# Sixteen loads of a tile replaced by one load, in an eight-core attention and feed-forward layer

## The chip, the cores and the metric

One Trainium2 chip, all 8 cores, one launch of one program. The time is device microseconds of the slowest core. Each core works alone on its share: core 0 to 3 take the first batch element, 4 to 7 the second, and every core owns 16 blocks of 128 query positions (2048 of 8192, interleaved among the four). Nothing is exchanged between cores; each one computes the keys and values of its whole batch element itself.

## The reference

One post-norm layer on x of shape (2, 8192, 2048): attention with a compressed key/value path, then a feed-forward part with int8 weights.

```
q   = x @ Wq                      # 16 heads of 128 + 64 (the 64 rotated by position)
c   = rmsnorm(x @ Wkv_a[:, :512]) # compressed keys and values
kr  = rope(x @ Wkv_a[:, 512:])    # 64 rotated key values, shared by the heads
k, v = c @ Wkv_b                  # 16 heads of 128 + 128
a   = causal_softmax(q . [k, kr] / sqrt(192)) @ v
x   = layernorm(x + a @ Wo)
g   = silu((x @ w_gate) * s_gate) * ((x @ w_up) * s_up)     # 8192 wide, int8 weights
out = layernorm(x + (g @ w_down) * s_down)
```

## The kernel before

Activations lie transposed: the 2048 features run over 16 chunks of 128 partitions, and 512 positions are the free dimension. A "tile" below is a buffer of 128 partitions x 8192 values in bf16, that is 16 chunks of 512 positions, chunk c in columns 512c to 512c + 511. Products are sums of 16 matmuls over these chunks.

The program has five stages. Each stage ends with a wait of SyncE for every DMA and for VectorE, and the next stage begins on all engines after it.

- A, queries: four input tiles `xb[tt]` (each core's own 2048 positions, from `xq` in f32) stay in SBUF; 24 blocks of query weights `wqb` pass by them. `load_xb` (L321) loads a tile. Tile 0 is loaded ahead of everything, then on the same queue come the casting of the output weights `wo_bf<-wo` (16 copies from DRAM to DRAM), the first query weights, and tiles 1 to 3 (L399). Results go to the scratch tensor `q_scr`.
- B, compressed keys and values: 16 tiles `xb2[par_x]` of the whole sequence (from `xf`, f32, rows of 8192 positions), in two buffers. The load of tile tt (L543) waits until TensorE has finished tile tt - 2, which is the rope block `propeB` of it (L562).
- C, attention: 16 heads by 4 groups of 512 queries. The result of head h and group gq, `ob_sb`, is stored to the scratch tensor `o_scr` (L889).
- D, output projection and first norm: for each gq the 16 heads' results are loaded from `o_scr` as a tile `osb` (L932, L943, from SyncE's queue); `osb` of gq + 1 is loaded at the start of gq once the buffer is free. For each of 16 output blocks weights `wob` and the residual `xtile` are loaded. The sum goes through a norm and to `h1_scr` in f32.
- E, feed-forward: four sweeps sw of 512 positions. Each loads the tile `h1b` from `h1_scr` (L1090, L1138; f32 in DRAM, bf16 in SBUF), runs 64 blocks of gate (L1107) and up (L1113) matmuls against it, then 16 blocks of down matmuls (L1157, 64 matmuls each, weights `wdb`), then transposes, norm and output. The load of `h1b` for the next sweep is written right behind the 64 blocks, waits for their last matmul, and stands in GpSimd's queue ahead of the down weights `wdb` of this sweep.

Loads that cast (all f32 and int8 sources) are issued by GpSimd, in program order; SyncE issues the others, ScalarE the stores to `h1_scr`. `P.dma` (L87) gives each queue four semaphores in turn. Successive DMAs of a queue share one until somebody waits for it; a wait always asks for the count of all DMAs issued on that semaphore so far (L62 to L84). So a wait for one DMA is a wait for the ones issued with it. All DMA issues carry the line of that helper (L101).

Of the kernel before, what the change touches and what calls it, by code (L numbers as in the profile page):

```python
# [9 lines left out]
BF16 = mybir.dt.bfloat16  # L10
# [9 lines left out]
OWN = NSLOT * 128  # L20
# [212 lines left out]
def build_nc(upto=5, dbg=()):  # L233
    nc = bass.Bass("TRN2", target_bir_lowering=False)
    dbg = set(dbg)

    t_xf = nc.dram_tensor("xf", [D, S], F32, kind="ExternalInput").ap()
    t_xq = nc.dram_tensor("xq", [D, OWN], F32, kind="ExternalInput").ap()
# [20 lines left out]
    t_out = nc.dram_tensor("out", [OWN, D], F32, kind="ExternalOutput").ap()  # L259

    q_scr = nc.dram_tensor("q_scr", [3072, OWN], BF16, kind="Internal").ap()
    o_scr = nc.dram_tensor("o_scr", [2048, OWN], BF16, kind="Internal").ap()
    h1_scr = nc.dram_tensor("h1_scr", [D, OWN], F32, kind="Internal").ap()
    wo_bf = nc.dram_tensor("wo_bf", [16, 128, 2048], BF16, kind="Internal").ap()

# [1 line left out]
    def dbg_out(name, shape, dtype):  # L267
        if name in dbg:
            dbg_aps[name] = nc.dram_tensor(
                "dbg_" + name, shape, dtype, kind="ExternalOutput").ap()  # L270
            return dbg_aps[name]
        return None
# [3 lines left out]
    d_krope = dbg_out("krope", [64, S], BF16)  # L276
    d_qmax = dbg_out("qmax", [1, 16], F32)
    d_krn = dbg_out("krn", [1, S], BF16)
    d_oscr = dbg_out("oscr", [2048, OWN], BF16)
    d_h1 = dbg_out("h1", [D, OWN], F32)  # L280
    d_kn15 = dbg_out("kn15", [128, S], BF16)
    d_vt15 = dbg_out("vt15", [128, S], BF16)
# [1 line left out]
    with ExitStack() as g:  # L284
        P = Prog(nc, g)
# [19 lines left out]
        with ExitStack() as a:  # L305
# [13 lines left out]
            pnR = [a.enter_context(nc.psum_tensor(f"pnR{i}", [128, 512], F32)) for i in range(2)]  # L319

            def load_xb(tt):  # L321
                return [P.dma("PL", xb[tt][:, 512 * c:512 * (c + 1)],
                              t_xq[128 * c:128 * (c + 1), 512 * tt:512 * (tt + 1)])
                        for c in range(16)]
            t_xb = {0: load_xb(0)}
            P.dma("SP", cosA[:, :], t_cos_own)
            t_trig = P.dma("SP", sinA[:, :], t_sin_own)
# [51 lines left out]
            for ocb in range(24):  # L379
# [4 lines left out]
                for tt in range(4):  # L384
                    bk = (4 * ocb + tt) % 4
                    par = tt % 2
                    for c in range(16):
                        waits = []
                        if c == 0:
                            waits = [t_w, t_xb[tt][15]] + bank_free[bk] + ([t_sel] if ocb == 0 else [])  # L390
                            bank_free[bk] = []
                        P.op("PE", lambda e, c=c, bk=bk, tt=tt, wpar=wpar: e.matmul(  # L392
                            pq[bk][:, :], wqb[wpar][:, 128 * c:128 * (c + 1)],
                            xb[tt][:, 512 * c:512 * (c + 1)],
                            start=(c == 0), stop=(c == 15)),
                            waits=waits, inc="pe" if c == 15 else None)
# [65 lines left out]
        with ExitStack() as bc:  # L462
# [5 lines left out]
            with ExitStack() as b:  # L468
# [71 lines left out]

                for tt in range(16):
                    par_x = tt % 2
                    t_x = [P.dma("PL", xb2[par_x][:, 512 * c:512 * (c + 1)],  # L543
                                 t_xf[128 * c:128 * (c + 1), 512 * tt:512 * (tt + 1)],
                                 waits=xb_free[par_x])
                           for c in range(16)]
                    xb_free[par_x] = []
                    t_cs = P.dma("SP", cosB[par_x][:, :],
                                 t_cosf[:, 512 * tt:512 * (tt + 1)], waits=cos_free[par_x])
# [4 lines left out]
                    for oc in range(5):  # L554
# [13 lines left out]
                        for c in range(16):  # L568
                            waits = []
                            if c == 0:  # L570
                                waits = [t_x[15], t_wk_ld[15]]
                                waits += (bank_free[par] if oc < 4 else rope_free)
                                if oc < 4:
                                    bank_free[par] = []
                                else:
                                    rope_free = []
                            P.op("PE", mk(c), waits=waits, inc="pe" if c == 15 else None)
# [54 lines left out]
            with ExitStack() as cph:  # L632
# [53 lines left out]
                for h in range(16):  # L686
# [98 lines left out]
                    for gq in range(4):  # L785
# [63 lines left out]
                        for it in range(niter):  # L849
# [27 lines left out]
                            if it % 2 == 1 and it + 3 < niter:  # L877
# [10 lines left out]
                            waits=ob_free[par_g], inc="dve")  # L888
                        ob_free[par_g] = []  # L889
                        po_free[par_g] = [("dve", tok_ob)]  # L890
                        t_ost = P.dma("SP", o_scr[128 * h:128 * (h + 1), 512 * gq:512 * (gq + 1)],
                                      ob_sb[par_g][:, :], waits=[("dve", tok_ob)], cls="st")
                        ob_free[par_g] = [t_ost]
                    kn_free = [("pe", P.cnt["pe"])]
# [15 lines left out]
        with ExitStack() as dph:  # L910
# [18 lines left out]
            osb_free = {0: [], 1: []}  # L929
            r1b_free = []  # L930
            t_o = {}
            t_o[0] = [P.dma("SP", osb[0][:, 512 * c:512 * (c + 1)],  # L932
                            o_scr[128 * c:128 * (c + 1), 0:512])
                      for c in range(16)]
            xt_free = {0: [], 1: []}
            o_free = []
            stat_free = []
# [3 lines left out]
            for gq in range(4):  # L941
                opar = gq % 2
                if gq + 1 < 4:  # L943
                    t_o[gq + 1] = [P.dma("SP", osb[(gq + 1) % 2][:, 512 * c:512 * (c + 1)],
                                         o_scr[128 * c:128 * (c + 1), 512 * (gq + 1):512 * (gq + 2)],
                                         waits=osb_free[(gq + 1) % 2] if c == 0 else ())
                                   for c in range(16)]
                    osb_free[(gq + 1) % 2] = []
                mm_toks = {}
                for oc in range(16):  # L950
# [9 lines left out]
                    for c in range(16):  # L960
                        waits = []
                        if c == 0:
                            waits = [t_o[gq][15], t_w] + bank_free[bk]
                            bank_free[bk] = []
                        P.op("PE", lambda e, c=c, oc=oc, bk=bk, wpar=wpar, opar=opar: e.matmul(  # L965
                            pwo[bk][:, :], wob[wpar][:, 128 * c:128 * (c + 1)],
                            osb[opar][:, 512 * c:512 * (c + 1)],
                            start=(c == 0), stop=(c == 15)),
                            waits=waits, inc="pe" if c == 15 else None)
# [72 lines left out]
        with ExitStack() as eph:  # L1042
# [43 lines left out]
            rtm_free = []  # L1086
            out_free = []
            out_stores = []
            t_h1map = {}
            t_h1map[0] = [P.dma("PL", h1b[:, 512 * c:512 * (c + 1)],  # L1090
                                h1_scr[128 * c:128 * (c + 1), 0:512])
                          for c in range(16)]
            for sw in range(4):
                t_h1 = t_h1map[sw]
                for ic in range(64):
# [4 lines left out]
                    for c in range(16):  # L1100
                        waits = []
                        if c == 0:
                            waits = [t_g, t_h1[15]] + gu_free[par] + (fuse_free if ic == 0 else [])
                            gu_free[par] = []
                            if ic == 0:
                                fuse_free = []
                        P.op("PE", lambda e, c=c, par=par: e.matmul(  # L1107
                            psG[par][:, :], wgb[par][:, 128 * c:128 * (c + 1)],
                            h1b[:, 512 * c:512 * (c + 1)],
                            start=(c == 0), stop=(c == 15)), waits=waits)  # L1110
# [24 lines left out]
                    tu_free[par] = [("dve", tok_f)]  # L1135
                tok_fuse_all = P.cnt["dve"]
                if sw + 1 < 4:
                    t_h1map[sw + 1] = [P.dma("PL", h1b[:, 512 * c:512 * (c + 1)],  # L1138
                                             h1_scr[128 * c:128 * (c + 1), 512 * (sw + 1):512 * (sw + 2)],
                                             waits=[("pe", P.cnt["pe"])] if c == 0 else ())  # L1140
                                       for c in range(16)]
                for oc in range(16):
                    par = oc % 2
                    t_wd_ld = P.dma("PL", wdb[par][:, :], t_wd[oc], waits=wd_free[par])
# [120 lines left out]
```

How the kernel before makes its waits and increments, by code:

```python
                def run(e, ops=ops):  # L124
                    for fn, waits, inc, n in ops:
                        for (s, v) in waits:
                            e.wait_ge(self.sem[s], v)
                        i = fn(e)
                        if inc is not None:
                            i.then_inc(self.sem[inc], n)
```

## Time and profile before

| | us |
|---|---|
| median of 2 runs | 8440.19 |
| lowest and highest of the runs | 8117.09, 8763.28 |
| the profiled execution | 8104.23 |
| its span on the slowest core (core 5) | 8102.7 |
| spans of the 8 cores | 8073.2 to 8102.7 |
| TensorE busy | 6631.2 (82%) |
| VectorE, ScalarE busy | 2568.9, 2592.2 (32% each) |
| GpSimd busy, DMA issues included | 608.3 (8%) |
| bytes moved by DMA | 639 MB, 79 GB/s on average |

Busy time is the time in which an engine had an instruction in work; matmuls overlap, so a busy TensorE isn't one at its peak. "DMA share" is the mean busy share of the core's 16 DMA engines; where several packets of an engine overlap it comes out above 1. GB/s counts the bytes written: a load that casts f32 to bf16 reads twice as much. "PEclk" is the granted TensorE clock, 1.00 for 2.4 GHz and 0.50 for 1.2 GHz.

### The profile page before, as it was taken

The numbers are of one execution on the slowest core, as the hardware profiler recorded it, in microseconds if no ns is written. First come the engines' busy times: TensorE is split into PE (matmuls) and PEld (weight loads), VectorE is DVE, ScalarE is ACT, GpSimd is POOL, SyncE is SP. The second block draws the span as 40 slices with busy tenths as digits, with TensorE's granted clock in tenths as the row PEclk, the third lists the DMA queues.
The fourth block names the chain that finished last, engine by engine and source line by source line (L and its number), as shares of the span: only waits on it lengthen the run. The fifth ranks groups of instructions, "written<-read, shape, count | busy, mean of one in ns | idle before, by whom it ended". The sixth has DMA issues, their size and how long they took to land. (4 is left out here: it accounts for less than half of the span.)

```text
span 8102.7 us, 101785 instructions; the slowest of 8 cores (8073.2 to 8102.7 us)
## 1 busy us (share of the span) xinstructions
PE 6631.2 (82%) x32368; PEld 2786.2 (34%) x32368; DVE 2568.9 (32%) x3876; ACT 2592.2 (32%) x3920; POOL 608.3 (8%) x1161
## 2 busy tenths in 40 slices
PE   3855958888888888888888745598989889988997
PEld 1322423333333333333333212244444444444443
DVE  0154444444444444444444222211021021102112
ACT  0201336555566665555555411000010000001000
POOL 2002400000000000000000001111011101100110
PEclk9977979999999999999999877799999999999999
DMA  8214720000000000000000243444444434443443
GB/s 110 63 31 74 118 44 9 9 7 8 8 9 9 9 8 9 9 9 8 8 9 9 88 128 124 124 154 152 157 144 155 160 140 152 146 171 137 154 162 132
DMA packets 236855, 639.37 MB, mean 79 GB/s; under 512 B 30320, under 2 KB 126704, under 8 KB 225008
## 3 DMA queue, kind: packets, MB, share of 16 engines
q0 software_dynamic: 159568, 530.98, 22.5%
q1 hardware_dynamic: 67552, 85.09, 3.3%
q10 hardware_dynamic: 9216, 16.78, 0.6%
q8 instruction: 277, 4.54, 0.2%
q14 instruction: 242, 1.98, 0.1%
HBM read 453.75 MB, written 62.91 MB: 64 GB/s over the span
## 5 line engine op out<-in xcount | busy, mean ns | idle before, releaser
L826 ACT ACTIVATE ptb<-poolC,bias_sb 128x512 bf16<-128x512 f32 x2560 | 1759.0, 687 | 724.9 <-PE poolC L817 350.0
L833 DVE SCALAR_TENSOR_TENSOR ptb<-qpos_sb,kposc_sb,ptb 128x512 bf16<-128x512 f32 x1024 | 769.2, 751 | 1452.4 <-ACT ptb L826 1366.9
L855 PE MATMUL poC<-ptb,vtm_sb 128*128 128x512 bf16 x2560 | 977.3, 382 | 223.8 <-DVE ptb L833 203.0
L1107 PE MATMUL psG<-h1b,wgb 128*128 128x512 bf16 x4096 | 936.3, 382 | 109.9 <-DMA wub<-wu 84.5
L865 PE MATMUL pdenC<-ptb,ones_mat 128*128 128x512 bf16 x2560 | 968.6, 378 | 0.0
L1157 PE MATMUL psD<-fuse,wdb 128*128 128x512 bf16 x4096 | 890.9, 381 | 65.1 <-DMA wdb<-wd 63.3
L1113 PE MATMUL psU<-h1b,wub 128*128 128x512 bf16 x4096 | 925.8, 379 | 0.0
L1121 ACT ACTIVATE tgE<-psG,sg_sb 128x512 bf16<-128x512 f32 x256 | 175.9, 687 | 1576.0 <-PE psU L1113 1576.0
L1126 DVE TENSOR_SCALAR tuE<-psU,su_sb 128x512 bf16<-128x512 f32 x256 | 192.1, 751 | 1458.3 <-PE psU L1113 1458.3
L1107 PEld LDWEIGHTS psG<-h1b,wgb 128*128 128x128 bf16 x4096 | 401.9, 98 | 604.5 <-issue 131.3
L1157 PEld LDWEIGHTS psD<-fuse,wdb 128*128 128x128 bf16 x4096 | 402.0, 98 | 554.0 <-issue 75.2
L1113 PEld LDWEIGHTS psU<-h1b,wub 128*128 128x128 bf16 x4096 | 400.8, 98 | 483.2
L855 PEld LDWEIGHTS poC<-ptb,vtm_sb 128*128 128x128 bf16 x2560 | 246.1, 96 | 857.7 <-issue 773.4
L813 PE MATMUL poolC<-qr_sb,krope_sb 64*128 64x512 bf16 x1280 | 494.8, 387 | 0.0
L817 PE MATMUL poolC<-qr_sb,krope_sb 64*128 64x512 bf16 x1280 | 494.8, 387 | 0.0
L803 PE MATMUL poolC<-qn_sb,knope_sb 128*128 128x512 bf16 x1280 | 485.3, 379 | 0.0
L810 PE MATMUL poolC<-qn_sb,knope_sb 128*128 128x512 bf16 x1280 | 484.8, 379 | 0.0
L392 PE MATMUL pqA<-xbA,wqb 128*128 128x512 bf16 x1536 | 360.6, 398 | 134.0 <-DMA wqb<-wq 105.2
L965 PE MATMUL pwo<-osb,wob 128*128 128x512 bf16 x1024 | 257.0, 413 | 249.7 <-DMA xtile<-xq 214.8
L1200 ACT ACTIVATE sq<-rtm 128x2048 f32<-128x2048 f32 x16 | 30.6, 1912 | 1038.3 <-DVE rtm L1191 1038.3
L1164 DVE SCALAR_TENSOR_TENSOR r<-psD,sd_sb,h1f 128x512 f32<-128x512 f32 x64 | 48.0, 751 | 905.8 <-PE psD L1157 905.8
L101 POOL DMA_DIRECT2D wob<-wo_bf x64 | 33.8, 528 | 3776.3 <-POOLq L133 3485.7
(137 smaller groups left out, 5428.4 us busy)
## 6 DMA issues: line engine op xcount, KB each, us to landing
wgb<-wg POOLq DMA_DIRECT2D x256, 512.0 KB, 3.4
wub<-wu POOLq DMA_DIRECT2D x256, 512.0 KB, 4.2
wdb<-wd POOLq DMA_DIRECT2D x64, 2048.0 KB, 7.6
xbB<-xf POOLq DMA_DIRECT2D x256, 128.0 KB, 7.0
wob<-wo_bf POOLq DMA_DIRECT2D x64, 512.0 KB, 3.9
xtile<-xq POOLq DMA_DIRECT2D x64, 256.0 KB, 4.3
h_scr<-h1t ACTq DMA_DIRECT2D x64, 256.0 KB, 2.5
h1f<-h_scr SPq DMA_DIRECT2D x64, 256.0 KB, 7.5
```

The lines of the kernel that those rows point to most:

```text
L392: P.op("PE", lambda e, c=c, bk=bk, tt=tt, wpar=wpar: e.matmul(pq[bk][:, :], wqb[wpar][:, 128 * c:128 * (c + 1)], xb[tt][:, 512 * c:512 * ( ...
L803: P.op("PE", lambda e, it=it0, bk=bk0, par_g=par_g: e.matmul(pool[bk][:, :], knope_sb[:, 128 * it:128 * (it + 1)], qn_sb[par_g][:, :], sta ...
L810: P.op("PE", lambda e, it=it1, bk=bk1, par_g=par_g: e.matmul(pool[bk][:, :], knope_sb[:, 128 * it:128 * (it + 1)], qn_sb[par_g][:, :], sta ...
L813: P.op("PE", lambda e, it=it0, bk=bk0, par_g=par_g: e.matmul(pool[bk][:, :], krope_sb[0:64, 128 * it:128 * (it + 1)], qr_sb[par_g][0:64, : ...
L817: tok = P.op("PE", lambda e, it=it1, bk=bk1, par_g=par_g: e.matmul(pool[bk][:, :], krope_sb[64:128, 128 * it:128 * (it + 1)], qr_sb[par_g] ...
L826: tok_e = P.op("ACT", lambda e, bk=bk: e.activation(ptb[bk][:, :], pool[bk][:, :], AF.Exp, bias=bias_sb[:, 0:1], scale=SSCALE), waits=[("p ...
L833: tok_m = P.op("DVE", lambda e, it=it, bk=bk, gq=gq: e.scalar_tensor_tensor(ptb[bk][:, :], qpos_sb[:, 512 * gq:512 * (gq + 1)], kposc_sb[: ...
L855: P.op("PE", lambda e, it=it, bk=bk, par_g=par_g, niter=niter: e.matmul(po[par_g][:, :], vtm_sb[:, 128 * it:128 * (it + 1)], ptb[bk][:, :] ...
L865: tok_pv = P.op("PE", lambda e, it=it, bk=bk, niter=niter: e.matmul(pden[:, :], ones_mat[:, :], ptb[bk][:, :], start=(it == 0), stop=(it = ...
L1107: P.op("PE", lambda e, c=c, par=par: e.matmul(psG[par][:, :], wgb[par][:, 128 * c:128 * (c + 1)], h1b[:, 512 * c:512 * (c + 1)], start=(c ...
L1113: P.op("PE", lambda e, c=c, par=par: e.matmul(psU[par][:, :], wub[par][:, 128 * c:128 * (c + 1)], h1b[:, 512 * c:512 * (c + 1)], start=(c ...
L1157: P.op("PE", lambda e, c=c, par=par: e.matmul(psD[par][:, :], wdb[par][:, 128 * c:128 * (c + 1)], fuse[:, 512 * c:512 * (c + 1)], start=(c ...
```

## The change

The tile loads in A, B, D and E are each written as one `dma_start` with a three-dimensional pattern (partition, chunk, position) in place of sixteen. In D the scratch tensor `o_scr` is laid out anew, group by partition by head by position, so that the part of one partition of a tile is one run of 16 KB. The stores into it keep their shape. The waits stay where they were.

```
-    o_scr = nc.dram_tensor("o_scr", [2048, OWN], BF16, kind="Internal").ap()
+    o_scr = nc.dram_tensor("o_scr", [4, 128, 16, 512], BF16, kind="Internal").ap()
...
             def load_xb(tt):
-                return [P.dma("PL", xb[tt][:, 512 * c:512 * (c + 1)],
-                              t_xq[128 * c:128 * (c + 1), 512 * tt:512 * (tt + 1)])
-                        for c in range(16)]
+                src = t_xq[:, 512 * tt:512 * (tt + 1)].rearrange(
+                    "(c p) q -> p c q", p=128)
+                dst = xb[tt][:, :].rearrange("p (c q) -> p c q", c=16)
+                return [P.dma("PL", dst, src)]
...
-                    t_x = [P.dma("PL", xb2[par_x][:, 512 * c:512 * (c + 1)],
-                                 t_xf[128 * c:128 * (c + 1), 512 * tt:512 * (tt + 1)],
-                                 waits=xb_free[par_x])
-                           for c in range(16)]
+                    t_x = [P.dma("PL", xb2[par_x][:, :].rearrange("p (c q) -> p c q", c=16),
+                                 t_xf[:, 512 * tt:512 * (tt + 1)].rearrange(
+                                     "(c p) q -> p c q", p=128),
+                                 waits=xb_free[par_x])]
...
-                        t_ost = P.dma("SP", o_scr[128 * h:128 * (h + 1), 512 * gq:512 * (gq + 1)],
+                        t_ost = P.dma("SP", o_scr[gq, :, h, :],
                                       ob_sb[par_g][:, :], waits=[("dve", tok_ob)], cls="st")
...
-            t_o[0] = [P.dma("SP", osb[0][:, 512 * c:512 * (c + 1)],
-                            o_scr[128 * c:128 * (c + 1), 0:512])
-                      for c in range(16)]
+            t_o[0] = [P.dma("SP", osb[0][:, :], o_scr[0])]
...
-                    t_o[gq + 1] = [P.dma("SP", osb[(gq + 1) % 2][:, 512 * c:512 * (c + 1)],
-                                         o_scr[128 * c:128 * (c + 1), 512 * (gq + 1):512 * (gq + 2)],
-                                         waits=osb_free[(gq + 1) % 2] if c == 0 else ())
-                                   for c in range(16)]
+                    t_o[gq + 1] = [P.dma("SP", osb[(gq + 1) % 2][:, :],
+                                         o_scr[gq + 1], waits=osb_free[(gq + 1) % 2])]
...
+            def load_h1b(sw, waits=()):
+                src = h1_scr[:, 512 * sw:512 * (sw + 1)].rearrange(
+                    "(c p) q -> p c q", p=128)
+                dst = h1b[:, :].rearrange("p (c q) -> p c q", c=16)
+                return [P.dma("PL", dst, src, waits=waits)]
             t_h1map = {}
-            t_h1map[0] = [P.dma("PL", h1b[:, 512 * c:512 * (c + 1)],
-                                h1_scr[128 * c:128 * (c + 1), 0:512])
-                          for c in range(16)]
+            t_h1map[0] = load_h1b(0)
...
-                    t_h1map[sw + 1] = [P.dma("PL", h1b[:, 512 * c:512 * (c + 1)],
-                                             h1_scr[128 * c:128 * (c + 1), 512 * (sw + 1):512 * (sw + 2)],
-                                             waits=[("pe", P.cnt["pe"])] if c == 0 else ())
-                                       for c in range(16)]
+                    t_h1map[sw + 1] = load_h1b(sw + 1, waits=[("pe", P.cnt["pe"])])
```

The four places that waited for piece 15 of a tile (`t_xb[tt][15]` and its like) now wait for the one load.

## Rows read from the trace of the kernel before

**Rows 1.** Windows A to E: length, busy us by engine, PEclk, DMA share, GB/s.
```profile
0.00:705.00 705.00, 400.25 (x1664) 166.97 (x1664) 235.72 (x443) 96.11 (x161) 55.96 (x115) 0.87 0.37 62
705.00:1060.00 355.00, 303.47 (x1360) 132.49 (x1360) 126.12 (x182) 107.54 (x177) 143.62 (x272) 0.92 0.72 108
1060.00:4552.00 3492.00, 2917.09 (x15648) 1119.32 (x15648) 1575.42 (x2320) 2066.81 (x3105) 2.12 (x4) 0.93 0.04 10
4552.00:5149.00 597.00, 288.15 (x1152) 117.06 (x1152) 136.12 (x197) 93.82 (x149) 68.82 (x130) 0.76 0.40 127
5149.00:8102.00 2953.00, 2722.22 (x12544) 1250.40 (x12544) 495.51 (x736) 227.95 (x328) 337.77 (x641) 0.96 0.43 151
```

**Rows 2.** Who waited for whom: us in total, times, longest us.
```profile
PE pwo L965 <- DMA xtile<-xq: 214.8, 33, 52.1
...
PE pqA L392 <- DMA wqb<-wq: 105.2, 1, 105.2
...
PE psG L1107 <- DMA wub<-wu: 84.5, 9, 75.7
...
PE psD L1157 <- DMA wdb<-wd: 63.3, 3, 21.2
...
PE pkvB L562 <- DMA xbB<-xf: 38.4, 1, 38.4
...
PE pwo L965 <- DMA osb<-o_scr: 33.6, 2, 29.6
...
PE pqA L392 <- DMA xbA<-xq: 28.7, 3, 11.1
```

**Rows 3.** Timeline in stage B: start us, us, instruction.
```profile
762.59 8.45 POOL L101 DMA_DIRECT2D xbB<-xf  x16 [28.73 <-PE propeB L562]
...
775.84 3.64 PE L562 MATMUL propeB<-xbB,wkva_sb 128*64 128x512 bf16 x16
...
780.70 13.99 PE L562 MATMUL pkvB<-xbB,wkva_sb 128*128 128x512 bf16 x64
```

**Rows 4.** Windows over one tile load in stage B.
```profile
766.00:771.00 5.00, 5.00 (x25) 2.26 (x24) 1.36 (x3) 2.06 (x4) 5.00 (x10) 1.00 1.13 154
771.00:778.00 7.00, 7.00 (x33) 3.18 (x32) 0.00 (x0) 2.37 (x4) 0.04 (x1) 1.00 1.16 197
778.00:781.00 3.00, 3.00 (x14) 1.14 (x13) 0.54 (x1) 0.94 (x2) 0.92 (x2) 1.00 0.02 3
```

**Rows 5.** Timeline between the up and the down matmuls of sweep 0.
```profile
5617.52 8.44 POOL L101 DMA_DIRECT2D h1b<-h_scr  x16 [12.75 <-PE psU L1113]
...
5625.82 1.20 POOL L101 DMA_DIRECT2D wdb<-wd  x2
...
5638.01 27.21 PE L1157 MATMUL psD<-fuse,wdb 128*128 128x512 bf16 x119 [21.07 <-DMA wdb<-wd]
```

**Rows 6.** Windows over the same stretch.
```profile
5619.00:5626.00 7.00, 0.00 (x0) 0.00 (x0) 0.00 (x0) 0.00 (x0) 7.00 (x15) 0.59 0.96 132
5626.00:5631.00 5.00, 0.00 (x0) 0.00 (x0) 0.00 (x0) 0.00 (x0) 1.02 (x2) 0.50 1.23 201
5631.00:5641.00 10.00, 2.99 (x8) 1.12 (x9) 0.00 (x0) 0.00 (x0) 0.00 (x0) 0.51 1.07 417
```

**Rows 7.** Groups of instructions: busy us, mean ns, idle before them.
```profile
L101 POOL DMA_DIRECT2D wdb<-wd x64 | 34.2, 542 | 801.3 <-PE psD L1157 785.4 <-issue 16.0
```

**Rows 8.** DMA queue of GpSimd from 5617 to 5643 us: packets, MB, share.
```profile
q0 software_dynamic: 2592, 6.29, 92.5%
```

**Rows 9.** Window in stage A, after the last of its tile loads was issued.
```profile
105.00:120.00 15.00, 6.55 (x16) 2.25 (x16) 0.00 (x0) 2.47 (x3) 0.53 (x1) 0.82 1.13 154
```

**Rows 10.** Window at the start of stage D, while its first loads flow.
```profile
4564.00:4575.00 11.00, 0.00 (x0) 0.00 (x0) 0.00 (x0) 0.00 (x0) 0.00 (x0) 0.50 1.05 342
```

**Rows 11.** The chain that ended last, at the start of stage E.
```profile
5149.27 6.97 POOL h1b L101 x14
...
5171.53 6.09 PE psG L1107 x16
```

More of the change, by code:

```diff
@@ L278, in build_nc @@
     d_krn = dbg_out("krn", [1, S], BF16)
-    d_oscr = dbg_out("oscr", [2048, OWN], BF16)
+    d_oscr = dbg_out("oscr", [4, 128, 16, 512], BF16)
     d_h1 = dbg_out("h1", [D, OWN], F32)
@@ L389, in build_nc @@
                         if c == 0:
-                            waits = [t_w, t_xb[tt][15]] + bank_free[bk] + ([t_sel] if ocb == 0 else [])
+                            waits = [t_w, t_xb[tt][-1]] + bank_free[bk] + ([t_sel] if ocb == 0 else [])
                             bank_free[bk] = []
@@ L570, in build_nc @@
                             if c == 0:
-                                waits = [t_x[15], t_wk_ld[15]]
+                                waits = [t_x[-1], t_wk_ld[15]]
                                 waits += (bank_free[par] if oc < 4 else rope_free)
@@ L962, in build_nc @@
                         if c == 0:
-                            waits = [t_o[gq][15], t_w] + bank_free[bk]
+                            waits = [t_o[gq][-1], t_w] + bank_free[bk]
                             bank_free[bk] = []
@@ L1102, in build_nc @@
                         if c == 0:
-                            waits = [t_g, t_h1[15]] + gu_free[par] + (fuse_free if ic == 0 else [])
+                            waits = [t_g, t_h1[-1]] + gu_free[par] + (fuse_free if ic == 0 else [])
                             gu_free[par] = []
```

## The prediction, made before the changed kernel ran

> **What bounds the kernel now.** I read the busy time by stage first [rows 1]. Five stages follow each other, each closed by a wait for everything: A (queries, 0 to 705 us), B (keys and values compressed, to 1060), C (attention, to 4552), D (output projection and first norm, to 5149), E (feed-forward, to 8102). TensorE is busy for 303 of 355 us in B and 2722 of 2953 us in E, so both are bound by it; C moves only 10 GB/s and has none of the changed loads; D has TensorE busy for 288 of 597 us and waits on other things. DMA is never the long-run bound: its share is 0.72 in B and 0.43 in E. A faster load can therefore only give back time in which TensorE stands still for it. The list of waits [rows 2] says how much there is: 105.2 us for the first query weights, 28.7 us in three waits for the next input tiles, 38.4 us for B's first tile, 33.6 us for the attention output in D, 63.3 us in three waits of 21 us between the two halves of a feed-forward sweep, and 75.7 us ahead of E. Of that last one only the part from 5149 us on is loads: E's loads are issued at 5149.3 us and TensorE starts at 5171.53 [rows 11], 22 us. The whole pool is about 290 us, 3.6% of the span, and most of it is the transfer itself.
>
> **What the change removes.** Every load of a 128 x 8192 tile in 16 pieces becomes one instruction: 4 tiles in A, 16 in B, 4 in E (from GpSimd's queue, f32 read and bf16 written), 4 in D (from SyncE's queue, bf16 both ways). That is 28 x 15 = 420 issues fewer. Bytes and the 2 KB reads of the f32 sources stay. The semaphores are picked and closed at the same points as before, because each wait already covered all 16 pieces. Each piece carries 16 packets beside its 128 rows: around the boundary in E 16 + 2 issues make 2592 packets [rows 8], 144 each, so a tile goes from 2304 to 2064 packets. In D the scratch tensor is laid out so that a partition's 16 KB are one run; the stores into it keep 128 rows of 1 KB.
>
> **GpSimd's issue time.** One piece holds GpSimd for 8.44 / 16 = 0.53 us [rows 3], and so does a down-weight load of 128 rows of 8 KB, 0.54 us [rows 7]: the size in bytes doesn't matter. All its issues have 128 rows, so no row shows what 2048 rows cost. The bounds are 0.53 us (per instruction) and 16 x 0.527 = 8.44 us, today's 16 issues together [rows 3, 5] (per row). It also isn't shown whether the first bytes move while the rest of the rows are still being written, as they do now between pieces. Call G the delay this puts before the first bytes. I take G small, below 3 us: an issue's cost hasn't followed its work so far. I keep 8.44 us for the range.
>
> **Stage B, hidden.** The load of a tile is issued at 762.59 us, when the tile two before it is done, and TensorE needs it at 780.70 us [rows 3]. Data flow from about 764 to 778.1 us: 154 GB/s up to 771, 197 GB/s after it, and a share of 0.02 from 778 on [rows 4]. So 14.1 us of transfer lie under 18.1 us of matmuls with 2.6 us to spare. What hides the load is the tile in between; 14 tiles repeat this (the first two are issued together). With G under 0.53 + 2.6 = 3.1 us nothing changes: 0 us. Without the cover every us of G costs 14 us. The first tile, behind the 16 loads of `wkva_sb` in the queue, is waited for: 0 to 10.4 - 14.1 = -4 us by the rates above and below, I take -1.
>
> **Stage E, exposed.** At the end of a gate/up half 16 pieces are issued from 5617.52 us, the first down weights at 5625.82 us, and TensorE starts at 5638.01 us after 21.07 us [rows 5]. The down weights share the queue and the semaphore with the 16 pieces, so TensorE waits for both. The engines move 132 GB/s during the issues, 201 GB/s from 5626 to 5631 us, then 417 GB/s, which are the down weights [rows 6]; the 2.1 MB tile is through at about 5631.4 us. The queue is backed up, not starved: a piece of 128 KB in 0.527 us would be 249 GB/s. Were the whole tile moved at 201 GB/s, it would take 10.4 us in place of 12.5: -2.1 us. Were the low rate the memory's, as in A, where 154 GB/s flow with GpSimd issuing only one load [rows 9], nothing is won. I take -1 us at each of four places (three boundaries and the start of E), -4 us together; bounds 0 and -8.4.
>
> **Stage A.** The queue is full: TensorE starts at 105.2 us behind the casting of the output weights and waits for the next three tiles [rows 2]. The load moves at 154 GB/s [rows 9] long after the last issue. Fewer packets: 0 us, at best 3 x 4 = 12 us off if these tiles ran at 201 GB/s (14 against 10.4 us). A large G would delay the very first bytes once: up to +8 us.
>
> **Stage D.** TensorE's first start waits for two attention tiles and the first weights, 5.8 MB, which flow at 342 GB/s in the steady part with 1 KB rows [rows 10]. With 16 KB rows at the best read rate seen (2 x 201 = 402 GB/s, since f32 is read for bf16) 4.2 MB take 10.4 us in place of 12.3: -2 us, bounds 0 and -4. The second wait for such a tile is 33.6 - 29.6 = 4.0 us [rows 2]; behind it TensorE waits up to 52.1 us for `xtile`, whose load waits for the norm's vector work, and that doesn't move: 0 us, bounds 0 and -4.
>
> **Sum.** B -1, E -4, A 0, D -2: -7 us. The profiled execution took 8104.2 us (span 8102.7), so 8097 us. The runs shown are 8117.1 and 8763.3 us; their median 8440.2 us is the mean of an undisturbed and a disturbed run, and I forecast the undisturbed time. Lower bound: -4 -8 -12 -8 = -32 us, 8072 us, and 13 us for the gap of 8104 to 8117 taken downwards: 8059.
>
> **Rivals.** *Late start, slower inside 2%.* The queue's rows are written one by one and the transfer starts only after the last: G = 8.44 us, 7.9 us more than now. In B the tile ends at 786.0 us, 5.3 us late; if the rate is then 201 GB/s throughout, 1.7 us late. Times 14: 24 to 74 us. TensorE then stands still long enough for its clock to fall as at the boundaries (0.50 in [rows 6]; the first 16 matmuls take 6.09 us [rows 11] where a quarter of 13.99 us [rows 3] is 3.50), up to 14 x 2.6 = 37 us more. E: 4 x (7.9 less 0 to 3.6) = 17 to 32; A and B's start 0 to 16. In all +41 to +159 us, middle +90: 8194 us. For it: the cost of one issue could be all rows. Against it: the cost of an issue has not moved with anything yet. It turns into a loss at G above 3.1 us.
>
> *Long generation, slower over 2%.* The same with rows that cost more in a three-dimensional pattern: each further us of G costs 14 (B) + 4 (E) + 2 = 20 us. At G = 20 us this is 90 + 11.6 x 20 = +320: 8424 us. It passes 2% (162 us) from G of about 12 us, 5.9 ns a row, where 527 ns / 128 = 4.1 ns is the most that today's issues can hold. No row speaks for it.
>
> *Slow reads, slower over 2%.* A DMA engine now reads 16 rows that lie 128 rows apart (4 MB apart in B's source, 1 MB in the others) where it read neighbours, and these fall on the same part of memory; the rate halves. B: 10.4 us become 20.8, or 14.1 become 28.2: 4.2 to 11.5 us late, x 14 = 59 to 161, clock up to 37. E: 4 x 10.4 to 14 = 42 to 56; A the same; B's first 10 to 14. +153 to +324, middle +220: 8324 us. Against it: across the 16 engines the rows read at one moment are spread as before. The Trainium skill (DMA: Bandwidth & Descriptors, Latency and other measured facts) has the rule behind this: copies whose rows are 4 MiB apart ran at half the rate of those 512 KiB apart. By it only B's source would suffer, +69 to +212 us from the terms above for B. No row here has such a stride.
>
> *Faster over 2%.* Each piece pays for its own start and end on the engines. The most the rows allow is 14.1 - 10.4 = 3.7 us at nine exposed tiles (A 4, B 1, E 4), 33 us: 8071 us. Over 2% would need 162 of the 290 us of waits. The Trainium skill (DMA: Bandwidth & Descriptors, Anatomy of one DMA and Rules for kernel authors) asks for coalescing, since a load costs about 2.0 us plus its bytes; by that, as an estimate from the page, 16 pieces of 256 KB would cost 42 us and one load 11.6 us, and nine such tiles would give 270 us back. The trace disagrees for loads queued together: [rows 4] have all 16 pieces through in 14 us.
>
> **How the numbers follow.** No change beyond small gains 0.50; late start 0.27; other shifts inside 2% 0.04; slow reads 0.09; long generation 0.08; faster over 2% 0.02. The likeliest gives 8097 us, with its own range 8059 to 8125. Small gains, late start and other shifts are the cases within 2% (about what a measurement of this kernel can tell from no change): 0.81. Slower by more 0.17, faster by more 0.02. The range takes the cases within 2%, from 8059 to 8104 + 159 = 8263 us.
>
> **What would show it.** GpSimd's span of one tile load against 8.44 us; TensorE's waits in B for the tile load (none if I am right, 14 of 2 to 6 us in the late start); the start of data after the issue, and the rate in B against 154 and 197 GB/s (about 100 with slow reads); the three waits for the down weights at 19 to 21 us, or near 28; D's first wait for `osb` at 26 to 30 us. A tile load with a span above 3.1 us before its first bytes, or a rate near 100 GB/s in B, would make the forecast wrong.

## The result, and the profile after

| | before | after |
|---|---|---|
| runs compared, us | 8096.4, 8103.1, 8111.6, 8117.1 | 8166.8, 8167.2, 8172.1, 8177.0 |
| profiled execution, span of the slowest core, us | 8102.7 (core 5) | 8175.4 (core 0) |
| spans of the 8 cores, us | 8073.2 to 8102.7 | 8124.9 to 8175.4 |

The ratio is 1.0079, 95% interval 1.0061 to 1.0096: the changed kernel is slower by 0.8%, about 64 us. The forecast was 8097 us and no change beyond small gains; 8170 us lie within 2% and within its range, but it is the sign that went wrong, and the runs below are about that. The times named are those of executions in which no die ran at a lower granted clock than the other, and the others (medians over all 8647.8 and 8491.4 us) say nothing here. One more execution of the changed kernel on record, 8157.0 us, isn't among those compared; with it the difference would be 61 us.

For every run below I took, core by core, the time from GpSimd's first instruction in a stage to its first in the next. The table has the median over the 8 cores of the profiled execution, in us:

| | A | B | C | D | E |
|---|---|---|---|---|---|
| before | 706.5 | 357.4 | 3487.8 | 579.3 | 2955.3 |
| after | 704.1 | 426.0 | 3488.8 | 576.2 | 2946.8 |
| difference | -2.4 | +68.6 | +1.0 | -3.1 | -8.5 |

The whole loss is in stage B. E gives a little back. D's length depends on how the cores happen to be staggered when they reach it: from core to core it took 567 to 593 us before and 568 to 602 us after.

The profile after, where it answers to the rows of before. First, who waited for whom on TensorE (columns: us in total, times, longest us), beside [rows 2]:

```profile
PE pwo L962 <- DMA xtile<-xq: 248.3, 34, 48.6
...
PE pqA L393 <- DMA wqb<-wq: 101.8, 1, 101.8
...
PE pkvB L563 <- DMA xbB<-xf: 99.9, 8, 47.9
...
PE psG L1107 <- DMA wub<-wu: 81.4, 5, 73.6
...
PE psD L1154 <- DMA wdb<-wd: 59.3, 3, 19.8
...
PE pqA L393 <- DMA xbA<-xq: 27.7, 3, 9.6
```

All are a little shorter but two. TensorE waits 99.9 us in eight waits for B's tiles where it waited once, 38.4 us (over the 8 cores 84.7 to 99.9 us, before 35.2 to 38.4). Its wait for `osb` is gone from core 0's list, and what it waits for at D's start, some 20 us, is now called `xtile`. So only the sum of the two compares: 248.4 us before on core 5, 248.3 us after on core 0, and 239 against 234 us as medians of the 8 cores.

The timeline of stage B, beside [rows 3] (start us, us, instruction, in brackets the wait before it):

```profile
765.94 1.15 POOL L101 DMA_DIRECT2D xbB<-xf  x1 [53.24 <-PE propeB L563]
...
783.43 1.14 POOL L101 DMA_DIRECT2D xbB<-xf  x1 [16.34 <-PE propeB L563]
...
789.46 16.35 PE L563 MATMUL pkvB<-xbB,wkva_sb 128*128 128x512 bf16 x63 [5.35 <-DMA xbB<-xf]
...
927.60 15.56 PE L563 MATMUL pkvB<-xbB,wkva_sb 128*128 128x512 bf16 x63 [11.75 <-DMA xbB<-xf]
```

The load is issued in 1.15 us, not 8.45, and yet TensorE starts 23.5 us after its issue where it had started after 18.1, having waited 5.35 us. Other tiles wait up to 12 us, and the matmuls of the four blocks after a wait take 16.35 in place of 13.99 us, at a granted clock of 0.88 (the window from 790 us below).

Windows over the same stretch, beside [rows 4] (length, busy us by engine, PEclk, DMA share, GB/s):

```profile
770.00:790.00 20.00, 14.60 (x65) 6.36 (x65) 6.27 (x10) 5.78 (x10) 1.14 (x1) 0.94 1.01 110
790.00:808.00 18.00, 17.95 (x74) 7.65 (x73) 2.31 (x4) 4.73 (x8) 0.00 (x0) 0.88 0.92 107
812.00:824.00 12.00, 11.95 (x57) 5.40 (x57) 6.40 (x9) 3.58 (x7) 0.00 (x0) 1.00 1.14 167
```

This is where the time went. The DMA engines are about as busy as before (share about 1) but move 107 to 110 GB/s in place of 154 to 197. What an engine has in work takes longer, for the same bytes and the same rows of 2 KB. And the rate isn't always low: for one tile, from 812 to 824 us, it is 167 GB/s. The rates of one core also vary with what the others move (last section), so the cleanest comparison is the stretch in which all 8 cores load their first two tiles. Core 0 from 724 to 740 us, before, after, and in the run e3_pad that follows below:

```profile
724.00:740.00 16.00, 4.88 (x15) 1.90 (x16) 0.00 (x0) 0.00 (x0) 5.42 (x11) 0.54 1.15 159
724.00:740.00 16.00, 0.00 (x0) 0.00 (x0) 0.00 (x0) 0.00 (x0) 0.00 (x0) 0.50 1.07 111
724.00:740.00 16.00, 4.41 (x12) 1.70 (x13) 0.00 (x0) 0.00 (x0) 0.00 (x0) 0.51 1.16 167
```

Over the 8 cores it is 157 to 171 GB/s before and 104 to 117 after: the rate is down by a third.

How long each tile load takes from issue to landing, minimum, median and maximum in us, after:

```profile
L101 POOL DMA_DIRECT2D xbB<-xf x16: 1140/1142/1300, 710.3 to 1067.4; - x16
...
DMA to landing us min/median/max: 18.8/27.9/48.8
```

The same for the tile of stage E, whose rows lie 1 MB apart:

```profile
L101 POOL DMA_DIRECT2D h1b<-h_scr x4: 1157/1158/1205, 5227.4 to 7164.2; - x4
...
DMA to landing us min/median/max: 13.7/14.0/15.8
```

Same shape in SBUF, same bytes, same issue cost, half the time (in E the cores don't all load at once, so the distance isn't the only difference). Last, the boundary in E, beside [rows 5] and [rows 6]:

```profile
5691.57 1.16 POOL L101 DMA_DIRECT2D h1b<-h_scr  x1 [13.06 <-PE psU L1113]
5692.72 1.08 POOL L101 DMA_DIRECT2D wdb<-wd  x2
5710.81 29.41 PE L1154 MATMUL psD<-fuse,wdb 128*128 128x512 bf16 x120 [19.85 <-DMA wdb<-wd]
```

The windows over it (columns as above):

```profile
5692.00:5702.00 10.00, 0.00 (x0) 0.00 (x0) 0.42 (x1) 0.00 (x0) 1.80 (x3) 0.69 1.01 158
5702.00:5712.00 10.00, 1.19 (x3) 0.43 (x4) 0.00 (x0) 0.00 (x0) 0.00 (x0) 0.50 1.12 387
```

The issues end 7 us earlier than before, and TensorE's wait is only 1.2 us shorter (19.85 against 21.07 us): the transfer was the wait.

### The profile page after: what moved, and what is told of

Its sections match the earlier page's. It is cut to its first block and busy times, and to the rows that moved or that the text cites. A ratio compares the mean times of both kernels' runs of the same rounds, so it can differ in the third digit from the quotient of the medians.

```text
span 8175.4 us, 100585 instructions; the slowest of 8 cores (8124.9 to 8175.4 us)
## 1 busy us (share of the span) xinstructions
PE 6602.6 (81%) x31798; PEld 2794.8 (34%) x32368; DVE 2569.0 (31%) x3876; ACT 2592.5 (32%) x3920; POOL 434.2 (5%) x801
## 5 line engine op out<-in xcount | busy, mean ns | idle before, releaser
L856 PE MATMUL poC<-ptb,vtm_sb 128*128 128x512 bf16 x2432 | 928.4, 382 | 218.0 <-DVE ptb L834 198.3
L811 PE MATMUL poolC<-qn_sb,knope_sb 128*128 128x512 bf16 x1280 | 484.8, 379 | 5.9 <-issue 2.5
L962 PE MATMUL pwo<-osb,wob 128*128 128x512 bf16 x1003 | 261.5, 421 | 250.0 <-DMA xtile<-xq 248.3
L804 PE MATMUL poolC<-qn_sb,knope_sb 128*128 128x512 bf16 x1200 | 454.9, 379 | 0.0
L563 PE MATMUL pkvB<-xbB,wkva_sb 128*128 128x512 bf16 x1003 | 235.9, 395 | 101.7 <-DMA xbB<-xf 99.9
## 6 DMA issues: line engine op xcount, KB each, us to landing
xbB<-xf POOLq DMA_DIRECT2D x16, 2048.0 KB, 27.9
```

The costliest lines, as they stand in the source:

```text
L804: P.op("PE", lambda e, it=it0, bk=bk0, par_g=par_g: e.matmul(pool[bk][:, :], knope_sb[:, 128 * it:128 * (it + 1)], qn_sb[par_g][:, :], sta ...
L811: P.op("PE", lambda e, it=it1, bk=bk1, par_g=par_g: e.matmul(pool[bk][:, :], knope_sb[:, 128 * it:128 * (it + 1)], qn_sb[par_g][:, :], sta ...
L856: P.op("PE", lambda e, it=it, bk=bk, par_g=par_g, niter=niter: e.matmul(po[par_g][:, :], vtm_sb[:, 128 * it:128 * (it + 1)], ptb[bk][:, :] ...
```

## The experiments

Three theories were set against each other. Theory 1: reads that follow each other a large power of two apart fall on the same part of memory. Theory 2: one large load is slow by itself, whatever it reads. Theory 3: far apart is slow because neighbouring rows share something in memory, power of two or not.

**e1_b_alone: is it B's loads alone?** From the kernel before, with one edit:

```
-                    t_x = [P.dma("PL", xb2[par_x][:, 512 * c:512 * (c + 1)], t_xf[128 * c: ...]) for c in range(16)]
+                    t_x = [P.dma("PL", ...rearrange("p (c q) -> p c q", c=16),
+                                 t_xf[...].rearrange("(c p) q -> p c q", p=128), ...)]
```

> Only the tile loads of stage B are one load each; A, D and E keep 16 pieces. Stage B took 357 us before and 426 us after the change (median over the cores). If B's loads alone are the loss: B 420 to 432 us, the other stages as before (E 2955 us, not 2947), total 8160 to 8180 us. If the loss comes from the stages together (the order in which cores reach B, or what A leaves behind): B below 400 us.

B took 412 to 450 us on the 8 cores, where 420 to 432 were expected, and 412, 413, 429 and 432 us on the four whose granted clock in B was the highest (0.89 to 0.91, as in the changed kernel; the others had 0.75 to 0.87). That clock makes its total, 8371.6 us, no measure of the edit, so B's length is what this run gives: the loss is there with nothing else changed.

**e2_all_but_b: and the rest?** The changed kernel with the 16 pieces back in B.

> A, D and E have one load per tile, B keeps 16 pieces. If B's loads alone are the loss: B 355 to 360 us, E 2946 us as in the changed kernel, A 2 us less than before, total 10 to 16 us less than before, ratio 0.998 to 0.999. If single loads cost something in every stage that contention hides: ratio 1.000 to 1.003.

B took 357.4 us, A 705.0, D 567.2, E 2950.3. Its total was 8085.8 and 8098.1 us against 8102.5 and 8117.2 us of the kernel before on the same chip: 0.2% less, which two runs a side support but don't measure well. So the change is a loss of about 69 us in B and a gain of 10 to 20 us elsewhere, E's share of it 5 us, A's 1.5 and D's 12, the last with the spread of D named above.

**e3_pad: theory 1 against the others.** The changed kernel, with B's source padded:

```
-    t_xf = nc.dram_tensor("xf", [D, S], F32, kind="ExternalInput").ap()
+    t_xf = nc.dram_tensor("xf", [D, S + 1024], F32, kind="ExternalInput").ap()
```

> The changed kernel, with 1024 unused columns behind each of the 2048 rows of B's source: rows lie 36 KB apart in place of 32 KB, and the 16 rows that one partition's load reads in turn lie 4.5 MB apart in place of 4 MB. Theory 1 (reads a large power of two apart fall on the same part of memory): B back to 355 to 365 us, rate in B above 150 GB/s. Theory 2 (one large load per tile is slow whatever it reads, because nothing spaces it): B stays at 418 to 433 us. Theory 3 (far apart is slow, power of two or not, because neighbouring rows share something open in memory): B stays at 418 to 433 us.

B took 358.7 us. One load a tile, the same 2048 rows in the same order, and the loss is gone; from 724 to 740 us the 8 cores move 156 to 168 GB/s. Issue to landing, on the slowest core:

```profile
L101 POOL DMA_DIRECT2D xbB<-xf x16: 1140/1141/1310, 717.7 to 1007.0; - x16
...
DMA to landing us min/median/max: 18.0/18.5/36.3
```

Medians over the cores lie between 15.0 and 18.5 us, against 25.6 to 27.9 us in the changed kernel. Theories 2 and 3 fall: the load is as large and its rows a little farther apart than before. Its total was 8092.0 us.

**e4_near and e13_near_pad: another order of rows.** The changed kernel with the features dealt the other way, so that a partition reads 16 neighbours (key weights laid out to match); then the same with the padded source.

```
-                                     "(c p) q -> p c q", p=128),
+                                     "(p c) q -> p c q", p=128),
```

> The changed kernel, with the features dealt to partitions the other way round: partition p reads rows 16p to 16p + 15, neighbours 32 KB apart, in one load (the key weights are laid out to match, so the sums are the same). Theory 1: B back to 355 to 365 us, unless the engines, which now work 2 MB apart from each other, meet in memory. Theory 2: B stays at 418 to 433 us. Theory 3: B back to 355 to 365 us. With the run before this one: fast and fast is theory 1, slow and slow theory 2, slow and fast theory 3.

> The single load of 16 neighbouring rows a partition (B took 366 to 375 us on the undisturbed die, 12 us more than the kernel before), now with the padded source: a partition's rows lie 36 KB apart, and the next partition's 576 KB further on in place of 512 KB. If the remaining 12 us come from powers of two between the partitions that the engines serve at one moment (theory 1 once more, across engines instead of within one): B 355 to 361 us. If they come from the order of the rows: B 366 to 375 us again.

Unpadded, B took 366.4 to 373.1 us (median 368.2) on cores 4 to 7, the ones at full clock throughout: most of the loss is gone, some 11 us remain, in two to six waits a core. The rate on the six cores that loaded from 724 to 740 us was 131 to 151 GB/s. Here a partition's reads lie 32 KB apart, but neighbouring partitions lie 512 KB apart. Padded, B took 358.6 us, 356.0 to 359.9 us over the cores, at 158 to 168 GB/s: the rest is gone too. So a distance of 512 KB between partitions costs something as well, and it is not the order of the rows.

**e5_four and e11_two: how many in turn?** Each tile in four loads of four chunks, or two of eight:

```
+                    t_x = [P.dma("PL", xb2[par_x][:, 2048 * g4:2048 * (g4 + 1)].rearrange("p (c q) -> p c q", c=4),
+                                 t_xf[512 * g4:512 * (g4 + 1), ...].rearrange("(c p) q -> p c q", p=128), ...)
+                           for g4 in range(4)]
```

> The changed kernel, with each tile of stage B loaded in four loads of four chunks: 4 MB apart within a load, but only four rows in turn before the next row is a neighbour. Theory 1 (an engine's successive reads a power of two apart share a part of memory): between the two, B 365 to 415 us, since three of four steps are still 4 MB. If what counts is only how many rows one load covers (2048 against 128): also between, so this run measures how the loss grows and does not tell the theories apart; if B is at 355 to 360 us, four steps in turn are too few to hurt.

> The changed kernel, each tile of stage B in two loads of eight chunks. With one chunk or four in turn B took 357 and 359 us, with sixteen 426 us. Theory 1 (what counts is how many reads in turn lie 4 MB apart, against how many an engine has under way at once): eight in turn is beyond four, B 365 to 415 us. If the loss belongs to the tile being one single load and has a threshold in the number of rows: B 357 to 360 us.

**e10_2mb and e8_pad32: how far apart, and how exact?** B's source as two halves of 4096 columns, so the reads in turn lie 2 MB apart; or with 32 columns of padding, so they lie 4 MB + 16 KB apart.

```
+    t_xf = nc.dram_tensor("xf", [2, D, S // 2], F32, kind="ExternalInput").ap()      # e10
+    t_xf = nc.dram_tensor("xf", [D, S + 32], F32, kind="ExternalInput").ap()         # e8
```

> The changed kernel with B's source stored as two halves of 4096 columns, so rows lie 16 KB apart and the sixteen reads in turn 2 MB apart in place of 4 MB; the transfer is otherwise the same. In A and E, where they lie 1 MB apart, no loss was seen. If the loss grows with the power of two: B 360 to 400 us. If 4 MB is the first bad distance: B 355 to 362 us. If any power of two in megabytes is equally bad and A and E only hide it: B 418 to 433 us.

> The changed kernel with 32 unused columns (128 bytes) behind each row of B's source in place of 1024: a partition's successive rows lie 4 MB + 16 KB apart. Theory 1 says only that the exact power of two is bad. If a step of 16 KB is enough to reach another part of memory: B 355 to 365 us. If memory is dealt out in larger portions: B between 370 and 433 us.

**e7_pad16: control.** The kernel before, 16 pieces, padded source.

> The kernel before with its 16 pieces a tile, but with the padded source (rows 36 KB apart). Control for the padded single load, where B took 358.7 us. If padding only undoes what the single load brought in: B 355 to 360 us, like the kernel before, and its first wait for a tile 35 to 38 us. If padding speeds up any reading of this source: the first wait for a tile below 33 us.

B took 355 to 360 us on the six cores with their full clock in B, and its first wait for a tile was 37.1 us against 38.4: padding alone brings nothing. All the runs on B together (one profiled execution each; B is the median over the cores, for e4 and e7 as said above; the rate is the lowest and highest of the cores from 724 to 740 us, without the two cores that reached B some 30 to 50 us late in e4, e7 and e8):

| rows in turn per partition | distance | B, us | GB/s, first tiles | GpSimd per issue, us |
|---|---|---|---|---|
| 1 (16 pieces) | | 357.4 | 157 to 171 | 0.61 (128 rows) |
| 1, padded | | 355 to 360 | 156 to 171 | 0.61 |
| 4 (4 loads) | 4 MB | 359.1 | 148 to 160 | 0.77 (512 rows) |
| 8 (2 loads) | 4 MB | 373.6 | 119 to 137 | 0.88 (1024 rows) |
| 16 (1 load) | 4 MB | 426.0 | 104 to 117 | 1.14 (2048 rows) |
| 16 | 4 MB + 16 KB | 366.1 | 128 to 171 | 1.14 |
| 16 | 4.5 MB | 358.7 | 156 to 168 | 1.14 |
| 16 | 2 MB | 359.2 | 155 to 165 | 1.14 |
| 16 | 32 KB (partitions 512 KB apart) | 366 to 373 | 131 to 151 | 1.14 |
| 16 | 36 KB (partitions 576 KB apart) | 358.6 | 158 to 168 | 1.14 |

Four in turn cost almost nothing: 359.1 us for B, hidden by its slack of 2.6 us [rows 4], and a rate some 4% lower. With eight there are waits again (on core 5 eight, 50.8 us, of them 42.3 for the first tile); with sixteen the rate is down by a third. The expectation of 365 to 415 us for four was too high: I had the loss grow with each step. 16 KB off the power of two take away seven eighths of the stage's loss (359 to 374 us from core to core), but not of the rate's: part of it is only hidden. At 2 MB B is as fast as before, though on one core the first tile, which isn't hidden, was waited for 45.5 us in place of 38. That run also brought neighbouring partitions from 32 to 16 KB apart, so it isn't the distance in turn alone. The totals of these runs, one each, were 8093.1 (e5), 8100.8 (e11), 8087.9 (e10) and 8095.7 us (e13); e8's 8132.2 and e7's 8212.8 us hold longer stages A and E on some cores (A up to 757 and 744 us), where these edits change nothing.

**e6_down_first, e9_down_own_sem and e12_down_16: the 20 us in E.** The list of waits after named a wait that the change had hardly touched: three times 20 us for the down weights, because their load stands behind the next sweep's tile in the queue. The three kernels issue the first two down weights during the gate and up blocks and the tile behind them.

```
+                    if ic in (56, 59):
+                        t_wd_pre[p2] = P.dma("PL", wdb[p2][:, :], t_wd[p2], waits=wd_free[p2], cls="wd")
...
-                if sw + 1 < 4:
-                    t_h1map[sw + 1] = load_h1b(sw + 1, waits=[("pe", P.cnt["pe"])])
...
+                    if oc == 1 and sw + 1 < 4:
+                        t_h1map[sw + 1] = load_h1b(sw + 1, waits=[("pe", tok_up_all)])
```

(`e6` has both at block 61 without `cls="wd"`, the semaphores of their own; `e6` and `e9` are on the padded single-load kernel, `e12` on the kernel before.)

> The changed kernel with the padded source, and in stage E the first two down weight loads of a sweep issued ahead of the tile for the next sweep, near the end of the gate and up blocks. If TensorE's 20 us at each of three boundaries are only the queue order: they vanish, E 2950 - 3 x 20 = 2890 us, less up to 3 x 2.6 us for the clock that no longer falls, total 8015 to 8035 us, ratio to before 0.989 to 0.992. If the tile load, now behind, delays the next down weights or the next sweep: E 2910 to 2950 us.

> The kernel before, 16 pieces everywhere, with only the order of stage E changed: the first two down weight loads are issued at blocks 56 and 59 on semaphores of their own, and the tile for the next sweep behind them. If the 21 us at three boundaries are the queue order alone: E 2955 - 3 x 21 = 2892 us, with up to 8 us more for the clock. If they need the single load too: E above 2910 us.

> The changed kernel with the padded source, and the same order in stage E. The earlier try lost 8.7 us at each boundary, since the weights of block 61 shared a semaphore with 4 MB of down weights. If that was all: no wait of TensorE for down weights, E 2885 to 2900 us, total 8020 to 8040 us, ratio to before 0.990 to 0.993. If the early loads still delay the gate and up weights: E 2900 to 2930 us.

e6 missed: E took 2932.4 us, in executions of 8063.4, 8069.0 and 8077.9 us. Its timeline (core 5) shows why, a wait of the gate matmuls for the down weights. The weights of that block were issued at 5565.11 us, ahead of the down weights, but share a semaphore with them:

```profile
5565.11 0.53 POOL L101 DMA_DIRECT2D wgb<-wg  x1 [6.19 <-PE psU L1119]
5566.15 1.08 POOL L101 DMA_DIRECT2D wdb<-wd  x2
...
5580.14 5.75 PE L1113 MATMUL psG<-h1b,wgb 128*128 128x512 bf16 x16 [8.72 <-DMA wdb<-wd]
...
5604.85 95.34 PE L1162 MATMUL psD<-fuse,wdb 128*128 128x512 bf16 x441 [1.69 <-DVE fuse L1137]
```

There are four such waits of about 9 us, one a sweep, nearly all of the 38 us by which e6 is behind e9. With semaphores of their own, and issued at blocks 56 and 59, E took 2894.3 us (e9) and, with 16 pieces, 2896.7 us (e12). Semaphores and blocks changed together; e6's lines speak for the semaphores, no run has them alone. In e9 the same timeline has a boundary 1.69 us wide, until VectorE's last product:

```profile
5594.78 1.16 POOL L103 DMA_DIRECT2D h1b<-h_scr  x1 [13.56 <-PE psU L1123]
5595.58 44.62 PE L1166 MATMUL psD<-fuse,wdb 128*128 128x512 bf16 x206 [1.69 <-DVE fuse L1141]
```

e9 took 8026.4 and 8036.5 us against 8098.4, 8101.9 and 8110.1 us of the kernel before on the same chip, 0.9% less. This is the version that beats both. e12's one run, 8046.5 us, says that most of that, 57 of 72 us, comes from the order of the queue and not from single loads.

## Why the prediction was wrong, point by point

- **The issue's cost (G small): right.** A single load holds GpSimd for 1.14 us where I allowed up to 3.1 us before anything would be late. *Late start* and *long generation* fall by that: the loads of 128, 512, 1024 and 2048 rows cost 0.61, 0.77, 0.88 and 1.14 us, about 0.28 ns for each further row, not 4.1. That the total also lies in the range of *late start*, +41 to +159 us, is chance, and so is that the forecast's range, drawn up to it, holds 8170 us.
- **Stage B (-1 us): wrong, +68.6 us, and this is the whole miss.** The step that failed is the one where the transfer was taken over unchanged: "Bytes and the 2 KB reads of the f32 sources stay", so 14.1 us under 18.1 us of cover. The cover was read rightly, with 2.6 us to spare; the transfer behind it wasn't the same. It went from 14.1 to 20 us and more a tile (2.1 MB at 107 GB/s are 19.6 us). The first tile, forecast at -1, is waited for 45.6 to 47.9 us on the 8 cores in place of 35.2 to 38.4. What the runs show in its place is that bytes and row length don't fix the time; the distance between the 16 reads in turn sets the rate: the same bytes and rows with 4.5 MB in place of 4 MB between them take B to 358.7 us.
- **The rival that came true was *slow reads*, at 0.09, and for B only.** Its mechanism was there, priced at +59 to +198 us for B's hidden tiles and +10 to +14 for the first; measured +68.6 in all. What I held against it, "across the 16 engines the rows read at one moment are spread as before", doesn't protect. The layout between partitions is as before, but the 16 reads that the pattern lists one after another for a partition aren't spread, and the table above shows that this is enough. The Trainium skill (DMA: Bandwidth & Descriptors, Latency and other measured facts) has rows 4 MiB apart at half the rate of rows 512 KiB apart and padding by 4 KiB as the cure; I cited it and gave it too little. Here the rate fell by a third, from 157 to 171 GB/s to 104 to 117, and 4 KB of padding a row cured it. The range I drew with that rule, +69 to +212 us with only B's source at fault, has the measured 68.6 us at its lower edge. Three things differ from that row of the Trainium skill, which is about the distance between partitions, where here it is the one between the reads of a partition: it has rows 2 MiB apart at 0.8 of the rate, where B at 2 MB moved 155 to 165 GB/s; it takes 512 KiB for the full rate, where 512 KB between partitions gave 131 to 151 GB/s; and it finds 192 bytes of padding useless, where 128 bytes a row (16 KB between the reads in turn) took away seven eighths of the stage's loss.
- **Stage E (-4, bounds 0 and -8.4): right in kind, a little small.** -8.5 us after, -5.0 in e2. As medians of the 8 cores the three boundaries went from 64.2 to 60.0 us together, the start of E from 22.1 to 19.2 us. TensorE's idle time there is mostly the transfer, and issuing faster couldn't shorten it much, as predicted.
- **The two rates of [rows 4] were read wrongly.** I took 154 GB/s for the rate during the issues and 201 for what a load could reach without them, and worked out the gains in A, B and E from that. A single padded load, with nothing issued beside it, shows two such rates as well (155 and 221 GB/s, last section), and between the two windows of [rows 4] the neighbouring core went from loading to nearly quiet.
- **Stage A (0): -2.4 us**, and 0 to -4 in the other runs with these loads. Its first query weights are waited for 101.3 to 101.9 in place of 103.4 to 105.2 us. Its three tiles are waited for 27.7 in place of 28.7 us; rows 1 MB apart cost nothing that shows.
- **Stage D (-2, bounds 0 and -4 for the start): the start went from 20.3 to 22.5 us down to 15.5 to 20.4 over the 8 cores** (medians 21.9 and 17.6), on core 2 from 22.5 to 15.8 at 379 GB/s with 16 KB runs against 342 [rows 10]. The other wait for `osb` shrank from 4 to 1 us. The sum had no term for SyncE's issues: the 32 pieces of the first two tiles held its queue for 19.80 us, the two loads for 0.80 (core 2, before and after). Longer runs and fewer issues came together, and no run separates them. Over the whole stage -3.1 us; in e2 -12, both within what D scatters from core to core.

```profile
4549.62 19.80 SPq L101 DMA_DIRECT2D osb<-o_scr  x32
...
4610.83 0.80 SPq L101 DMA_DIRECT2D osb<-o_scr  x2
```

- **No pay by the piece: right.** *Faster over 2%*, and with it the estimate of 270 us from the 2.0 us a load of the Trainium skill (DMA: Bandwidth & Descriptors, Anatomy of one DMA), has no support: with 15 of 16 issues gone the three boundaries lost about 1.4 us each.

## What to carry to other kernels

When one load replaces several, the order of reads inside it changes even if its bytes don't: write down the distance between two reads that the pattern makes in turn for a partition, and the one between partitions, and if either is a large power of two (4 MB in turn and 512 KB between partitions cost here, 1 and 2 MB in turn did not), try padding the row or keep the pieces. A count of issues says little where the queue is backed up anyway; what it does say is where in the queue a large transfer stands, and moving that one transfer behind the loads that are needed first gave 56 to 59 us in stage E here, in either form.

## What the runs showed of the hardware that I had not expected

- A load's cost on GpSimd grows by only about 0.28 ns a row: 0.61 us for 128 rows, 1.14 us for 2048.
- The slow reads need many in turn: 4 reads 4 MB apart after each other cost almost nothing (148 to 160 against 157 to 171 GB/s), 8 cost 16 us over stage B (119 to 137 GB/s), 16 cost 69 us (104 to 117 GB/s). That would fit an engine having several reads under way at once, which no view here shows, as none shows the order in which an engine makes them; what in the memory they collide on is open as well.
- The rate of a load also goes with what a neighbouring core moves, and not only at the slow distance. In the kernel before, core 5's 154 and 197 GB/s [rows 4] stand beside 191 and 49 GB/s of core 4:

```profile
766.00:771.00 5.00, 5.00 (x25) 2.17 (x23) 0.00 (x0) 1.69 (x3) 0.00 (x0) 1.00 1.18 191
771.00:778.00 7.00, 7.00 (x33) 3.00 (x32) 2.72 (x4) 2.58 (x5) 3.48 (x7) 1.00 0.36 49
```

In e3_pad cores 0 to 3 show from 764 to 768 us:

```profile
764.00:768.00 4.00, 3.95 (x20) 1.80 (x19) 0.00 (x0) 1.18 (x2) 0.00 (x0) 1.00 1.23 221
764.00:768.00 4.00, 4.00 (x20) 1.78 (x19) 3.48 (x6) 1.18 (x2) 0.65 (x1) 1.00 0.38 46
764.00:768.00 4.00, 4.00 (x19) 1.67 (x17) 0.00 (x0) 1.18 (x2) 0.00 (x0) 1.00 1.10 155
764.00:768.00 4.00, 4.00 (x20) 1.84 (x19) 0.00 (x0) 1.18 (x2) 0.00 (x0) 1.00 1.16 155
```

Core 0 loads at 221 GB/s while core 1 moves 46, and cores 2 and 3, both loading, get 155 each. In the changed kernel it is the same on a lower level: core 0 moved 110 and 107 GB/s while core 1 moved 98 and 118, and 167 GB/s from 812 to 824 us while core 1 moved 49. Each core's windows are counted from its own start, so this takes it that the cores started together, and no run was made to test it.
